# Group 0 of a sparse expert layer: split token rows, searches behind the one-hot tiles, pads first

## The reference

```python
topk_w, topk_ids = _grouped_topk(x @ gate_w, bias)       # 6 of 64 experts
flat_e = topk_ids.reshape(-1); order = jnp.argsort(flat_e); se = flat_e[order]
pos = jnp.arange(Tn * K) - jnp.searchsorted(se, se, side='left')
valid = pos < CAP                                        # CAP = 48 per expert
buf = zeros((E, CAP + 1, H)).at[se, slot].set(x[tok])[:, :CAP]
h = silu(einsum('ech,ehf->ecf', buf, w_gate)) * einsum('ech,ehf->ecf', buf, w_up)
out = einsum('ecf,efh->ech', h, w_down)                  # H = 256, F = 96
y = segment_sum(gathered * w, tok)                       # plus a shared expert
```

## Time and profile before

| | |
|---|---|
| time, median of 3 runs | 431.84 us (431.19 to 432.56) |
| the profiled execution | 430.28 us, of it a span of 428.3 us |
| busy PE, DVE | 399.0 us (93%), 352.2 us (82%) |
| busy ACT, POOL | 220.5 us (51%), 118.8 us (28%) |
| chain that ended last | PE 49%, DVE 40%, issue 4%, ACT 3% |
| granted clock of PE, mean | 0.995 of full speed |

### The profile page before, as it was taken

One profiled execution on the slowest core, in us unless ns is written; L12 is line 12 of the kernel. 1 busy time (PEld: TensorE's weight loads), 2 busy tenths in 40 slices (PEclk: granted clock), 3 DMA queues, 4 the chain that ended last, 5 costly groups with the idle time before them and its releaser, 6 DMA issues.

```text
span 428.3 us, 5191 instructions
## 1 busy us (share of the span) xinstructions
PE 399.0 (93%) x1711; PEld 216.3 (50%) x1715; DVE 352.2 (82%) x655; ACT 220.5 (51%) x410; POOL 118.8 (28%) x85
## 2 busy tenths in 40 slices
PE   5899999899998789989999999999999999998795
PEld 2244545687655557767777754344444344333241
DVE  4999999898699889999979799437977977638996
ACT  3976838742484468646668564511111141146892
POOL 2722007000000563321200000337684845540000
PEclk9999999999999999999999999999999999999899
DMA  7950001900096459767764510720000000000002
GB/s 262 399 219 2 2 0 35 390 5 2 9 346 189 98 140 314 214 213 253 233 215 142 201 51 1 300 93 2 0 0 1 0 2 0 0 0 0 1 2 98
DMA packets 12251, 47.45 MB, mean 111 GB/s; under 512 B 2897, under 2 KB 5434, under 8 KB 9794
## 3 DMA queue, kind: packets, MB, share of 16 engines
q1 hardware_dynamic: 11074, 43.20, 28.7%
q0 software_dynamic: 1152, 3.93, 3.8%
HBM read 44.76 MB, written 2.37 MB: 110 GB/s over the span
## 4 chain that ended last, share of the span: by engine, by line
PE 49%; DVE 40%; issue 4%; ACT 3%; DMA 1%; another core or an unknown queue 1%; POOL 1%; POOLq 0%; SPq 0%; DVEq 0%; ACTq 0%
PE bank L1668 8%; PE bank L1804 8%; PE bank L1791 6%; PE bank L1724 4%; PE bank L1836 4%; PE bank L1833 4%; PE bank L1697 3%; PE bank L1635 2%; DVE wkv_b L806 2%; DVE wkv_b L795 2%; DVE wkv_a L795 2%; PE bank L1759 2%; PE bank L1566 2%; DVE wkv_c L773 1%; DVE wkv_a L806 1%
## 5 line engine op out<-in xcount | busy, mean ns | idle before, releaser
L730 ACT ACTIVATE early<-bank 128x512 f32<-128x512 f32 (+1 forms) x24 | 14.3, 597 | 86.0 <-PE bank L1804 76.6
L1668 PE MATMUL bank<-onehot,rows 128*128 128x512 f32 x192 | 52.0, 410 | 0.0
L1307 DVE TENSOR_TENSOR early<-early,bank 128x512 f32<-128x512 f32 (+1 forms) x24 | 16.4, 684 | 36.2 <-ACT early L730 32.8
L420 POOL DMA_INDIRECT arena<-token_rows,arena x24 | 26.3, 1098 | 62.8 <-PE bank L1706 32.7
L1804 PE MATMUL bank<-arena 128*128 128x512 f32 (+1 forms) x96 | 42.2, 600 | 0.1
L431 POOL TENSOR_TENSOR early<-early,arena 128x512 f32<-128x512 f32 (+1 forms) x12 | 20.1, 1672 | 76.0 <-DMA arena<-pair_weights 67.8
L1668 PEld LDWEIGHTS bank<-onehot,rows 128*128 128x128 f32 x192 | 34.0, 188 | 11.0 <-issue 4.1
L1791 PE MATMUL bank<-cT,arena 128*128 128x512 f32 x80 | 37.9, 596 | 0.0
L437 POOL TENSOR_TENSOR early<-early,arena 128x512 f32<-128x512 f32 x10 | 22.3, 2231 | 28.2 <-DVE early L1307 28.2
L1804 PEld LDWEIGHTS bank<-arena 128*128 128x128 f32 (+1 forms) x96 | 15.7, 181 | 22.6 <-issue 20.7
L1697 PE MATMUL bank<-arena 128*64 128x192 f32 x256 | 22.5, 329 | 2.3 <-issue 2.3
(11 more groups left out here) (399 smaller groups left out, 893.6 us busy)
## 6 DMA issues: line engine op xcount, KB each, us to landing
arena<-in_w_gateup SPq DMA_DIRECT2D x16, 768.0 KB, 7.7
arena<-in_w_down SPq DMA_DIRECT2D x8, 768.0 KB, 10.5
arena<-in_wq SPq DMA_DIRECT2D x1, 2048.0 KB
arena<-in_wo SPq DMA_DIRECT2D x1, 2048.0 KB, 8.0
const<-in_const SPq DMA_DIRECT2D x1, 1688.0 KB, 10.5
arena<-in_w_upgate SPq DMA_DIRECT2D x1, 1408.0 KB, 5.8
kT<-in_kT SPq DMA_DIRECT2D x2, 512.0 KB, 5.6
xT<-in_xT SPq DMA_DIRECT2D x1, 1024.0 KB, 8.8
```

The lines of the kernel that those rows point to most:

```text
L420: g.indirect_dma_start(xg[:, t % XRING, :], None, scratch[:, :], bass.IndirectOffsetOnAxis(ap=toki[:, t:t + 1].bitcast(U32), axis=0)).then ...
L1668: return mm(bank[2 * ct + ch][:], rows1[:, i % RRING, part, ct * P:(ct + 1) * P], onehot1[:, t, ch * CHUNK:(ch + 1) * CHUNK], start=False, ...
```

## The change

- Token rows of group 0: ACT copies `ctok1` as float32r into `tok_hi` (it lies in `rows1`, free until group 0's slot copies); POOL writes the remainder to `tok_lo` (in the place of `ratio1`, free at this time); `first_rows` multiplies both parts with the one-hot tile as float32r matmuls.
- DVE builds all eight one-hot tiles first, with the reciprocal behind the sixth; the six searches follow. The three slot matmuls move behind `gate_up(0)` and write bank 3 instead of bank 4.
- POOL clears the pads as soon as the rows of group 0 are complete and before all gathers. The write of `w1` to the table counts on `small1_in`, so ACT's copy of group 0's rows no longer waits for it; POOL still does.
- Group 0: the hidden is turned ahead of `shared_down`; `down(0)` runs before `rows_in(1)`; group 1's rows go to banks 4 and 5 instead of 6 and 7; DVE's `shared_product` and two scans move behind the first products; ACT's `euk(2)` moves from ahead of group 0's rows to behind its second hidden copy, and `scaled(3, 0)` from group 0 to group 1, ahead of `guess_log(2)`. `idle(6, 1)` becomes `idle(4, 2)`, filling matmuls.
- Layer 3: `gu3(2)` moves ahead of the last `down2`.

```diff
@@ -107,7 +107,11 @@
         xT, kT, ekT, ekvT, cT = (sb(n, [P, CT, N]) for n in ("xT", "kT", "ekT", "ekvT", "cT"))
-        ratio = [sb(f"ratio{i}", [P, CT, N]) for i in range(2)]
+        ratio = [sb("ratio0", [P, CT, N])]
+        split_rows = nc.sbuf_tensor("tok_low", [P, NT, C], F32R)
+        tok_lo = split_rows.__enter__()
+        split_rows.__exit__(None, None, None)
+        ratio.append(sb("ratio1", [P, CT, N]))
         wA, wB, wC, wD = (sb(n, [P, CT, N]) for n in ("wkv_a", "wkv_b", "wkv_c", "wkv_d"))
@@ -128,6 +132,7 @@
         rows1 = sb("rows1", [P, RRING, 2, C], F32R)
+        tok_hi = rows1[:].rearrange("p a b c -> p (a b c)").rearrange("p (t c) -> p t c", t=NT)
         first1 = onehot1[:].rearrange("p t n -> p (t n)").rearrange("p (t e r) -> p t e r", e=GE, r=CAP)
@@ -326,7 +331,7 @@
             sp.wait_ge(S("w1_ready"), 1)
-            sp.dma_start(scratch[0:N, C:ROW].rearrange("(t p) c -> p t c", p=P), w1).then_inc(S("rows_out"), 16)
+            sp.dma_start(scratch[0:N, C:ROW].rearrange("(t p) c -> p t c", p=P), w1).then_inc(S("small1_in"), 16)
             for g in range(2, NG):
@@ -404,14 +409,18 @@
             g.memset(h1, 0.0).then_inc(S("pads_ready"), 1)
+            for j in range(NT // 2):
+                pool.wait_ge(S("ctok1_ready"), NT // 2 + j + 1)
+                two = slice(2 * j, 2 * j + 2)
+                g.tensor_tensor(tok_lo[:, two, :], ctok1[:, two, :], tok_hi[:, two, :].bitcast(F32), ALU.subtract).then_inc(S("pads_ready"), 1)
+            pool.wait_ge(S("xgT_done"), 1)
+            pool.wait_ge(S("rows_out"), 32)
+            for i in range(2):
+                last = g.memset(xgT[i][:, :, GS:XW], 0.0)
+            last.then_inc(S("pads_ready"), 1)
             pool.wait_ge(S("toki_ready"), 1)
-            pool.wait_ge(S("rows_out"), 48)
+            pool.wait_ge(S("small1_in"), 96)
             for t in (*range(GT, 2 * GT), *range(GT), *range(2 * GT, ST)):
-                if t == 0:
-                    pool.wait_ge(S("xgT_done"), 1)
-                    for i in range(2):
-                        last = g.memset(xgT[i][:, :, GS:XW], 0.0)
-                    last.then_inc(S("pads_ready"), 1)
                 if t % GT == 0 and t >= 2 * GT:
@@ -624,11 +633,16 @@
                 s.activation(shg[:, j * CHUNK:(j + 1) * CHUNK], bank[4 + 3 * j][0:F1, :], ACT.Silu).then_inc(S("shg_ready"), 1)
+            act.wait_ge(S("shu_done"), 2)
             act.wait_ge(S("picked1"), 1)
+            for j in range(NT // 2):
+                act.wait_ge(S("ctok1_ready"), j + 1)
+                s.activation(tok_hi[:, 2 * j:2 * j + 2, :], ctok1[:, 2 * j:2 * j + 2, :], ACT.Copy).then_inc(S("ctok1_ready"), 1)
+            act.wait_ge(S("picked1"), 2)
             for t in range(NT):
...
             last.then_inc(S("ws1_ready"), 1)
-            act.wait_ge(S("picked1"), 2)
+            act.wait_ge(S("picked1"), 3)
             for t in range(NT):
@@ -637,10 +651,10 @@
                     if g == 0:
-                        act.wait_ge(S("rows_out"), 48)
+                        act.wait_ge(S("rows_out"), 32)
                     if g >= 2:
                         act.wait_ge(S("gu1_done"), 2 * g - 2)
-                    s.copy(xgT[g % 2][:, ct, 0:GS], bank[6 + ct if g else 3 + 2 * ct][:, 0:GS]).then_inc(S("xgT_ready"), 1)
+                    s.copy(xgT[g % 2][:, ct, 0:GS], bank[(3 + 2 * ct, 4 + ct, 6 + ct)[min(g, 2)]][:, 0:GS]).then_inc(S("xgT_ready"), 1)
@@ -658,16 +672,18 @@
-            euk(2)
             rows_in(0)
...
                 hidden_copy(g, 0)
-                if g < NG - 1:
+                if 0 < g < NG - 1:
                     rows_in(g + 1)
...
                 if g == 0:
+                    euk(2)
+                    rows_in(1)
+                if g == 1:
                     scaled(3, 0)
@@ -1018,8 +1034,9 @@
             scores = bank[5][:].rearrange("p (q h e) -> p h q e", h=2, e=E1)
-            step(v.tensor_tensor(sb1.rearrange("p (h q) e -> p h q e", h=2), scores,
-                                 bias1.unsqueeze(1).unsqueeze(1).to_broadcast([P, 2, NT // 2, E1]), ALU.add))
+            v.tensor_tensor(sb1.rearrange("p (h q) e -> p h q e", h=2), scores,
+                            bias1.unsqueeze(1).unsqueeze(1).to_broadcast([P, 2, NT // 2, E1]), ALU.add).then_inc(S("picked1"), 1)
+            dve.wait_ge(S("picked1"), 1)
@@ -1069,18 +1086,17 @@
             dve.wait_ge(S("cm1_ready"), 1)
-            first_onehot(0)
-            first_onehot(1)
+            for t in range(NT):
+                first_onehot(t)
+                if t == 5:
+                    dve.wait_ge(S("ws1_ready"), 1)
+                    step(v.reciprocal(wr1, ws1))
+                    v.engine_nop().then_inc(S("picked1"), 1)
             dve.wait_ge(S("counts1_done"), 3)
...
                                    last_two[:, 0:CHUNK + CAP])
-                if r < 5:
-                    first_onehot(r + 2)
                 if r == 2:
-                    dve.wait_ge(S("ws1_ready"), 1)
-                    step(v.reciprocal(wr1, ws1))
-                    v.engine_nop().then_inc(S("picked1"), 1)
                     dve.wait_ge(S("counts1_done"), 4)
@@ -1089,9 +1105,8 @@
             step(v.tensor_copy(dec2, dec[:, 2 * CT:3 * CT, :]))
-            first_onehot(7)
             dve.wait_ge(S("counts1_done"), 5)
-            slots = bank[4][:, 0:ST].rearrange("p (t g) -> p t g", t=GT)
+            slots = bank[3][:, 0:ST].rearrange("p (t g) -> p t g", t=GT)
             v.tensor_scalar(toki.bitcast(U32).rearrange("p (g t) -> p t g", t=GT), slots,
@@ -1102,10 +1117,6 @@
-            shared_product(0)
-            shared_product(1)
-            back_again(2, 0, 0, near=1)
-            forth(2, 0, 1, near=1)
@@ -1145,6 +1156,10 @@
                 if g == 0:
+                    shared_product(0)
+                    shared_product(1)
+                    back_again(2, 0, 0, near=1)
+                    forth(2, 0, 1, near=1)
                     back_again(2, 0, 1, near=1)
@@ -1631,18 +1646,15 @@
                 pe.wait_ge(S("first_ready"), t + 1)
+                pe.wait_ge(S("pads_ready"), 3 + t // 2)
                 for ct in range(CT):
-                    last = mm(bank[3 + 2 * ct][:, 0:GS], ctok1[:, t, ct * P:(ct + 1) * P],
-                              first1[:, t].rearrange("p e r -> p (e r)").bitcast(F32), start=(t == 0), stop=(t == NT - 1))
+                    for part in range(2):
+                        last = mm(bank[3 + 2 * ct][:, 0:GS], (tok_hi, tok_lo)[part][:, t, ct * P:(ct + 1) * P],
+                                  first1[:, t].rearrange("p e r -> p (e r)"), start=(t == 0 and part == 0), stop=(t == NT - 1 and part == 1))
                 return last
...
                 first_rows(t)
-            pe.wait_ge(S("mk1_ready"), 2)
-            for t in range(GT):
-                last = mm(bank[4][:, t * NG:(t + 1) * NG], spreadv[:].rearrange("e g c -> e (g c)")[:, t * P:(t + 1) * P], groups1[:],
-                          start=True, stop=True)
-            last.then_inc(S("counts1_done"), 1)
@@ -1654,10 +1666,12 @@
                     pe.wait_ge(S("outw_ready"), GT * (g - 1))
+                else:
+                    pe.wait_ge(S("h1_ready"), 2)
                 for t in range(GT):
...
                     for ct in range(CT):
-                        last = tr(bank[6 + ct][:, t * P:(t + 1) * P], xg[:, i % XRING, ct * P:(ct + 1) * P], ident)
+                        last = tr(bank[(4 if g == 1 else 6) + ct][:, t * P:(t + 1) * P], xg[:, i % XRING, ct * P:(ct + 1) * P], ident)
                 last.then_inc(S("xgT_done"), 1)
@@ -1687,8 +1701,7 @@
                 if g == 0:
-                    pe.wait_ge(S("pads_ready"), 3)
-                    pe.wait_ge(S("toki_ready"), 2)
+                    pe.wait_ge(S("pads_ready"), 3 + NT // 2)
                     pe.wait_ge(S("shg_ready"), 2)
@@ -1709,9 +1722,9 @@
                 r = ring[g % 2]
-                if g < NG - 1:
+                if 0 < g < NG - 1:
                     pe.wait_ge(S("xgT_ready"), 2 * g + 4)
-                else:
+                elif g:
                     pe.wait_ge(S("outw_ready"), GT * g)
@@ -1726,17 +1739,23 @@
-            idle(6, 1)
+            idle(4, 2)
             gate_up(0)
+            pe.wait_ge(S("mk1_ready"), 2)
+            for t in range(GT):
+                last = mm(bank[3][:, t * NG:(t + 1) * NG], spreadv[:].rearrange("e g c -> e (g c)")[:, t * P:(t + 1) * P], groups1[:],
+                          start=True, stop=True)
+            last.then_inc(S("counts1_done"), 1)
+            turn_hidden(0, 0)
+            turn_hidden(0, 1)
             shared_down(0, 0)
             shared_down(0, 1)
-            turn_hidden(0, 0)
-            turn_hidden(0, 1)
+            down(0)
             rows_in(1)
-            down(0)
             for g in range(1, NG):
...
                 if g == 1:
+                    pe.wait_ge(S("toki_ready"), 2)
```

(2 more changed lines are left out.)

## The result

The changed kernel takes 436.74 us (median of 13 runs, 433.56 to 439.12); the kernel before took 431.51 us beside it (13 runs). The ratio is 1.0111, 95% interval 1.0081 to 1.0142: about 4.8 us slower, where I had forecast 2.0, and above the 436.0 us at which my range ended. The profiled execution has a span of 435.2 us (436.98 us with what lies around it), 6.9 us longer than before's.

A forecast was written before the change was run, and what follows sets the result against it. Bound: a chain through PE's one-hot matmuls from 131.9 us, then DVE without idle from 161 to 187 us. ACT's chain +2.2 and the moved pair -0.25 make +1.95 us: 431.84 to 433.8 us, range 430.5 to 436.0.

The forecast's parts named there:

- The lock, 139.9 and 145.2: DVE's one-hots and POOL's subtractions hold each other out; token rows complete at 139.9 us, slot numbers at 145.2.
- The rule of the Trainium skill that I had weighed: Split-row matmuls: weight load overlaps only in another row group, giving 8.5 us; 6.2 us at 0.193 each was taken instead.
- landing took under 4.3 us ... I take no wait; the bound is 2.2 us: Group 0's last gather done at about 152.9 us, rows wanted by DVE at 155.0; no wait, at most 2.2 us.
- Rival C: Gathers late by up to 2.2 us, or POOL's subtractions at 3.25 us each; about 436.5 us, chance 0.10.
- The gap for Silu goes, because gate and up end 0.8 us before the slot numbers: Group 0 on DVE: its 2.43 us of idle for the second Silu disappears.
- ACT's chain in group 1, +1.9 to 2.8 us: Eight scalings, 3.30 us, moved ahead of the Ln delay slot copies to 169.7 us; DVE loses 2.2, passed on in full.
- The 0.9 us in front of the slot copies: Group 1 on ACT: slot copies start 0.9 us later than 169.7 if the 0.91 us is ACT's own.
- The second copy of the hidden ends at about 163.1, as before: Group 1 on ACT: the hidden's second copy, ahead of the Ln, ends unchanged at about 163.1 us.
- The moved pair, -0.25 us: Layer 3: third pair fills PE's 0.79 us gap, Gelu early, DVE's masked sum next late; -0.25 us, bounds -0.4 and +0.1.
- The side: Whole kernel against about 0.3% (1.3 us): slower by more 0.55, within 0.30, faster by more 0.15.

The follow-up runs named there:

- e5: Changed kernel with the one-hot tiles' mask in a PSUM bank instead of SBUF, so each tile reads one SBUF tensor; 437.42 us, ratio 1.0137.
- e7: Changed kernel without the split: whole float32 token rows, no rounding copies on ACT, no subtractions on POOL; 443.36 us, ratio 1.0249.
- e1: Changed kernel with SP issuing group 2's weights only after group 2's gathered rows have landed; 432.87 us, ratio 1.0068.
- e8: Kernel before with only layer 3's third gate pair moved ahead of layer 2's last down; one profiled execution, the pair giving 0.0 at the bias.
- e3: Changed kernel with ACT's scaled(3, 0) moved back to group 0; 435.59 us, ratio 1.0124.
- e6: Changed kernel with the edits of e1, e3 and e5 together; 432.05 us, ratio 0.9986.
- e9: e6 plus two idle matmul pairs, ahead of the first turned hidden rows and ahead of the shared down; 432.88 us, ratio 1.0011.
- e16: Changed kernel with five matmuls that add zeros on PE ahead of group 0's first scatter; 441.3 us, ratio 1.0182.
- e17: e14 without the two idle matmul pairs; 432.78 us, ratio 1.0005.
- e15: Changed kernel with ten matmuls that add zeros on PE ahead of group 0's first scatter; 440.99 us, ratio 1.0201.
- e14: e9 with 68 already met waits in ACT's program between 100 and 114 us; 430.12 us, ratio 0.9958.
- e13: Kernel before with 68 already met waits in ACT's program between 100 and 114 us; 431.63 us, ratio 0.9997.
- e4: Changed kernel with the edits of e1 and e3 together; 434.16 us, ratio 1.0056.
- e18: e17 with group 2's gathers held until ACT has copied group 1's rows; 432.32 us, ratio 1.0017.
- e10: e9 with 64 already met waits in ACT's program near 95 us; 431.46 us, ratio 1.002.

## Why the prediction was wrong

*The lock, 139.9 and 145.2:* right in mechanism and size (139.67 and 144.67; e5 and e7 show the lock itself). A matmul with its weight load takes 0.177 us where I took 0.193 (in e5 the second starts at 132.47, the 32nd at 137.77). The rule of the Trainium skill that I had weighed (TensorE: Matmul & The Clock Gate, Part 3, The mechanism: a load overlaps only in another row group) doesn't agree with that pace.

*"landing took under 4.3 us ... I take no wait; the bound is 2.2 us":* this step failed. The landing time was taken from a stretch where the DMA engines were lightly loaded (shares of 0.44, 0.36 and 0.13 from 148 to 154 us in before), and I had moved down(0) 4.7 us forward without asking what it releases: SP's weights, which in before started at 156.99, 3.3 us after DVE had taken the rows, and now start at 151.48, before the last gather of group 0 is issued. Rival C had gathers that land late, at up to 2.2 us and 0.10; the wait was 3.88 us, 0.40 without the collision (e1). What followed from it, 1.9 us on PE by group 2's late rows and by the half clock, was in no rival. That C's total, 436.5, is near the 436.74 measured is luck: its terms were POOL's subtractions at 3.25 us each (1.61 at most here) and 2.2 us for the rows.

*"The gap for Silu goes, because gate and up end 0.8 us before the slot numbers":* it went, but its larger part wasn't PE's. In before the second Silu started 1.7 us after gate and up were through, and e8's profile has 0.82 us in place of before's 2.43 with the same program up to there.

*ACT's chain in group 1, +1.9 to 2.8 us:* right in kind. With the collision away (e1) the slot copies start at 169.71 (forecast 169.7), the waits for them are 1.18, 0.31 and 0.30 us, and DVE's scan behind them is 1.8 us later than before's (172.36 against 170.53), where I took 2.2. The whole of e1 is +2.9 us by the ratio, 2.05 by the medians and 1.7 by the spans, against 1.95 forecast: that agrees, but not as closely as the medians alone make it look. In the changed kernel itself they cost less (0.46 us and the two small ones; e3's profile gains 1.3, its runs nothing), since DVE waits for PE's scatter at the same time. The 0.9 us in front of the slot copies, which I had left open, is not ACT's own: they follow the Ln at 174.93 with no idle time.

*"The second copy of the hidden ends at about 163.1, as before":* 168.51, all of it from the collision and the clock; 163.29 in e1.

*The moved pair, -0.25 us:* the gap went, next late was DVE's sum as I wrote, and it took nearly all: 0.0 at the bias (e8).

*The side:* slower, in part from ACT's chain as forecast. Of the 6.9 us between the two profiles 1.7 are left in e1, and 5.2 come from the collision and the clock behind it, which I had not priced. Between the ratios it is 2.9 and 1.9 of 4.8 us.

What stays open: what ACT waits for in its stand-stills. They occurred in seven profiles, each in a stretch in which gathers are issued: 5.4 to 12.5 us of idle in e5, e6, e7, e9, e16 and e17, of which 3.0 to 6.7 us come after PE had finished what ACT needed, and 2.57 us in before, of which 1.7. And the clock's price in the changed kernel, about 1 us of the 1.9, is read from two traces; e15 and e16 did not isolate it.

## What to carry to other kernels

When a step is moved forward, list what its end releases, buffers first, and look what the transfers that then start will meet; a landing time holds only for the DMA load it was read under. Where PE's new timeline has stretches of half-empty work, price the half clock that may follow, and try idle matmuls there: here the long runs went with them (e6 to e9, e17 to e14), though only e14 is faster than before, by 0.4%. Before a gap that has closed is put down to an edit, look whether it also closes in another execution of the same program (e8 against e13). Compare distributions of runs, not only medians, when two or three such events come and go between executions.

## What the runs showed of the hardware that I had not expected

- The last gather of group 0, beside 2.3 MB of weights, was usable 5.8 us after its issue ended; with the weights held back, 2.4 us after (e1: 152.84 and 155.19).
- A float32r matmul of 384 columns with weights of its own runs at a pace of 0.177 us; the same columns in float32 took 0.33 (e7: 32 in 10.59 us).
- ACT can stand still for 3.0 to 6.7 us after the last thing that it is known to need, in a stretch where POOL issues gathers (e5, e6, e7, e9, e16, e17); SP's start is late too where it can be told (2.2 us in e5). Of one and the same program up to there, one profile has it and another not (before and e8, e16 and the changed kernel).
- In or behind the same thin stretch of PE, between 142 and 148 us, the granted clock fell to 0.50 in some executions (e4, e6, e15, e18) and stayed at 1.00 in others (the changed kernel's profile, e1, e17). With two idle pairs in it, e9's, e10's and e14's profiles keep 1.00 there; behind the stretch at 156 to 160 us e14's falls to 0.57 for 4 us.
- 64 waits that are already met, ahead of a wait for DVE, made ACT load its table behind that wait (99.32 us in e10) and not ahead of it (91.06 in e9).
